# Two heads in one operand tile: scores of the first attention in 64x32 tiles of different halves of the array

## What is computed

```python
xn = _layernorm(x, axis=-1)
x = x + _L0_attn_ref(xn, ...) + _L0_ffn_ref(xn, ...)

# first branch: 16 heads of width 8, rotary positions, causal
scores = jnp.einsum('bqhd,bkhd->bhqk', q, k) / math.sqrt(Hd)
scores = jnp.where(causal, jnp.finfo(scores.dtype).min, scores)
attn = jax.nn.softmax(scores, axis=-1)
out = jnp.einsum('bhqk,bhkd->bhqd', attn, v)

# second branch: 6 nodes after each other, each an attention of 8 heads of width 16, not causal
o = _mha(q, k, v, Wq[c], Wk[c], Wv[c], Wo[c])
nodes[c] = act_w[c] * o + q
```

## Time and profile before

| | |
|---|---|
| median of 3 runs | 1426.18 us (1425.83 to 1427.39) |
| profiled execution | 1423.05 us, its span 1421.3 us |
| PE busy | 1380.5 us, 97% of the span |
| DVE busy | 1263.0 us, 89% |
| ACT busy | 1139.5 us, 80% |
| POOL busy | 449.8 us, 32% |

### The profile page before, as it was taken

The page is one execution under the profiler, slowest core; times in us unless marked ns, Lnnn a source line. Parts: engine busy times, 40 slices in busy tenths (PEclk is TensorE's granted clock), DMA queues, the critical chain, the costliest instruction groups (busy, mean ns, idle before and its releaser), DMA issues.

```text
span 1421.3 us, 60282 instructions
## 1 busy us (share of the span) xinstructions
PE 1380.5 (97%) x26216; PEld 935.3 (66%) x26216; DVE 1263.0 (89%) x1587; ACT 1139.5 (80%) x2133; POOL 449.8 (32%) x936
## 2 busy tenths in 40 slices
PE   6899999999999999999999999999999999999995
PEld 4467777656667666676676766766667666667652
DVE  8889999999989989899899898988989989989895
ACT  3378887688878878888788887887888878878784
POOL 5141115324422433233423332234233432330210
PEclk9899999999999999999999999999999999999998
DMA  8131112343232422333323323233233332321211
GB/s 253 47 116 60 51 59 98 119 142 119 81 127 70 132 97 77 102 109 107 104 78 114 107 74 121 83 123 107 69 101 107 101 107 80 127 98 56 76 38 40
DMA packets 115668, 137.68 MB, mean 97 GB/s; under 512 B 14972, under 2 KB 90109, under 8 KB 115277
## 3 DMA queue, kind: packets, MB, share of 16 engines
q1 hardware_dynamic: 115405, 133.83, 28.7%
HBM read 64.63 MB, written 61.98 MB: 89 GB/s over the span
## 4 chain that ended last, share of the span: by engine, by line
PE 88%; DMA 4%; DVE 3%; SPq 2%; ACT 1%; POOL 1%; issue 1%; ACTq 0%; POOLq 0%; DVEq 0%
PE s L1069 53%; PE cps L1163 26%; PE misc L1069 7%; DMA qs<-mrows 2%; DVE neg_max L971 1%; SPq L431 1%; PE misc L1064 1%; ACT probs L784 1%; DMA dram_raw_b<-csb 1%; PE s L1064 0%; DVE s L967 0%; POOL parts L601 0%; POOL ks L596 0%; POOL full L614 0%; SPq L500 0%
## 5 line engine op out<-in xcount | busy, mean ns | idle before, releaser
L784 ACT ACTIVATE probs<-s 128x512 f32<-128x512 f32 x1792 | 1059.2, 599 | 227.4 <-PE s L1069 166.8
L971 DVE TENSOR_REDUCE neg_max<-s 128x1 f32<-128x1024 f32 x768 | 936.5, 1222 | 62.0 <-PE s L1069 9.1
L1069 PE MATMUL s<-qs,ks 99*32 99x512 bf16 (+2 forms) x7680 | 808.4, 370 | 7.1 <-DMA qs<-mrows 5.1
L1069 PE MATMUL s<-ks,qs 96*32 96x512 bf16 (+2 forms) x7680 | 606.5, 369 | 6.3 <-DMA ks<-dram_qk_a 2.7
L1163 PE MATMUL cps<-probs,vs 128*32 128x256 f32 (+1 forms) x7552 | 591.4, 368 | 0.6 <-ACT probs L784 0.6
L1069 PEld LDWEIGHTS s<-qs,ks 99*32 99x32 bf16 x7680 | 235.8, 94 | 240.6 <-ACT probs L784 96.7
L1163 PEld LDWEIGHTS cps<-probs,vs 128*32 128x32 f32 x7552 | 316.4, 110 | 76.3 <-issue 17.0
L1069 PEld LDWEIGHTS s<-ks,qs 96*32 96x32 bf16 x7680 | 292.5, 97 | 88.6 <-issue 24.5
L633 POOL TENSOR_TENSOR mparts<-neg_max,zeros 128x8 bf16<-128x8 f32 x128 | 26.0, 203 | 796.0 <-DVE neg_max L971 654.3
L967 DVE CUSTOM_DVE_ANT_0 s<-s,mask_q 128x1024 f32<-128x1024 f32 (+7 forms) x256 | 187.8, 785 | 23.5 <-PE s L1069 14.8
L706 POOL TENSOR_TENSOR parts<-full,zeros 128x512 bf16<-128x512 f32 x48 | 61.4, 1280 | 52.2 <-DVE full L949 52.2
(11 more groups left out here) (134 smaller groups left out, 607.6 us busy)
## 6 DMA issues: line engine op xcount, KB each, us to landing
dram_qk_b<-parts SPq DMA_DIRECT2D x48, 384.0 KB, 3.2
qs<-dram_qk_b SPq DMA_DIRECT2D x96, 192.0 KB
ks<-dram_qk_b SPq DMA_DIRECT2D x96, 192.0 KB
dram_qk_b<-parts SPq DMA_DIRECT2D x48, 256.0 KB, 3.2
dram_raw_b<-csb SPq DMA_DIRECT2D x93, 128.0 KB, 4.3
dram_qk_b<-parts SPq DMA_DIRECT2D x48, 128.0 KB, 3.2
vsrc<-srcT SPq DMA_DIRECT2D x12, 512.0 KB, 3.1
ctx_b<-dram_raw_b SPq DMA_DIRECT2D x44, 128.0 KB
```

The lines of the kernel that those rows point to most:

```text
L784: nc.scalar.activation(buf[:, lo:hi], s2[bank][:, 0:hi - lo], ACT.Exp, scale=scale).then_inc(exp_done, 1)
L971: last = ve.tensor_reduce(peak, scores, AX.X, ALU.max, negate=True)
L1069: last = te.matmul(dst[c0:c0 + STRIP, :], lhsT[:, c0:c0 + STRIP], rhs, start=start, stop=stop, tile_position=(0, c0))
```

## The change

Head k and head k+2 of A share one operand tile. There are two such tiles of q (`qa`) and two of k (`ka`, laid over `ctx_b`, which is unused until B). Unit k lies in tile k % 2, in rows 0 to 50 or 64 to 114 (`first_row`): 48 rows of data and 3 for the maximum. Both scores of A are now strips of 64 rows and 32 columns, with `tile_position=(row, c0)`. Because units k and k-2 lie in different halves, the scores by query and by key of one step use different rows of the array. The mask on the diagonal can read only the 64 rows of its half; it takes the 32 columns of the identity in that half, and for output rows of the other half one of two further masks (`mask_far`). Operands of B, contexts and the transpose stay as they are. The data that DMAs move stays the same.

At the start, DVE clears no longer `qs` and `ks` but sets `ka` to ones; POOL writes the ones of `ks` before it waits for the statistics instead of at the end of its constants, and makes the two further masks.

```diff
+ROWS_A = 6 * DA
+HALF_ROWS = 64
...
+        mask_far = [sb(f"mask_far{n}", [128, 128], BF16) for n in range(2)]
+        qa = [sb(f"qa{n}", [128, S], BF16) for n in range(2)]
...
+        ka = [ctx_b[:, n * CH:(n + 1) * CH].bitcast(BF16) for n in range(2)]
...
+        def first_row(which, k):
+            return HALF_ROWS * (k % RING // 2) if which == "A" else 0
+        def operands(which, k):
+            return (qa[k % 2], ka[k % 2]) if which == "A" else (qs[k % RING], ks[k % RING])
+        def data_rows(which, k):
+            row = first_row(which, k)
+            return slice(row, row + (ROWS_A if which == "A" else KROW))
+        def score_rows(which, k):
+            row = first_row(which, k)
+            return slice(row, row + (ROWS_A if which == "A" else KROW) + 3)
...
-            sp.wait_ge(dve_const, 3 * RING)
+            sp.wait_ge(dve_const, RING + 2)
...
+            for s in range(RING):
+                pool.wait_ge(pool_const, 8 + s)
+                pl.memset(ks[s][MROW:128, :], 1.0).then_inc(pool_const, 1)
+            pool.wait_ge(pool_const, 8 + RING)
             for n in range(NB):
                 pool.wait_ge(ln_stats, n + 1)
...
+            for mask, key_of_row_0 in ((mask_k, 0), (mask_far[0], HALF_ROWS), (mask_far[1], -HALF_ROWS)):
+                pl.affine_select(out=mask[:, :], in_=mask[:, :], pattern=[[1, 128]], compare_op=ALU.is_ge,
+                                 fill=MASKED, base=-key_of_row_0, channel_multiplier=-1).then_inc(pool_const, 1)
...
-            for s in range(RING):
-                pool.wait_ge(pool_const, N_CONST - RING + s)
-                pl.memset(ks[s][MROW:128, :], 1.0).then_inc(pool_const, 1)
...
             for s in range(RING):
-                for ring in (qs[s][:, :], ks[s][:, :], vs[s][:, :, :]):
-                    ve.memset(ring, 0.0).then_inc(dve_const, 1)
+                ve.memset(vs[s][:, :, :], 0.0).then_inc(dve_const, 1)
+            for n in range(2):
+                ve.memset(ka[n][:, :], 1.0).then_inc(dve_const, 1)
...
-            def mm_strips(dst, lhsT, rhs, start=True, stop=True):
+            def mm_strips(dst, lhsT, rhs, start=True, stop=True, row=0):
                 for c0 in range(0, 128, STRIP):
                     last = te.matmul(dst[c0:c0 + STRIP, :], lhsT[:, c0:c0 + STRIP], rhs, start=start, stop=stop,
-                                     tile_position=(0, c0))
+                                     tile_position=(row, c0))
                 return last
+            def mask_strips(dst, row):
+                rows = slice(row, row + HALF_ROWS)
+                for c0 in range(0, 128, STRIP):
+                    here = c0 // HALF_ROWS == row // HALF_ROWS
+                    at, mask = (c0, mask_k) if here else ((c0 + HALF_ROWS) % 128, mask_far[row // HALF_ROWS])
+                    last = te.matmul(dst[c0:c0 + STRIP, :], ident_h[rows, at:at + STRIP], mask[rows, :],
+                                     start=False, stop=True, tile_position=(row, c0))
+                return last
...
-                    last = mm_strips(bank[:, first - lo:end - lo], ky[0:KALL, t * 128:(t + 1) * 128],
-                                     q[0:KALL, q0 + first - at:q0 + end - at], stop=not diagonal)
+                    last = mm_strips(bank[:, first - lo:end - lo], ky[rows, t * 128:(t + 1) * 128],
+                                     q[rows, q0 + first - at:q0 + end - at], stop=not diagonal, row=row)
                     if diagonal:
-                        last = mm_strips(bank[:, at - lo:at - lo + 128], ident_h[:, :], mask_k[:, :],
-                                         start=False)
+                        last = mask_strips(bank[:, at - lo:at - lo + 128], row)
...
-                                    last = mm_strips(s1[n % 2][:, lo:hi], q[0:KROW, t * 128:(t + 1) * 128],
-                                              ky[0:KROW, lo - at:hi - at])
+                                    last = mm_strips(s1[n % 2][:, lo:hi], q[rows, t * 128:(t + 1) * 128],
+                                                     ky[rows, lo - at:hi - at], row=row)
```

More of the change, by code:

```diff
@@ L197 @@
 FINISH = [(0, TB)] + [(TB + t0, tiles) for t0, tiles in LATE_TILES]
-N_CONST = 12 + 2 * RING
+N_CONST = 20 + RING
 def added(kind, r, k):
@@ L359, in head_row, with max_rows @@
             return here * HB + k if 0 <= k < UP else other * HB + k % UP
+        def first_row(which, k):
[8 more added lines that the diff above has]
+            return slice(row, row + (ROWS_A if which == "A" else KROW) + 3)
+        def max_rows(which, k):
+            return slice(data_rows(which, k).stop, score_rows(which, k).stop)
         block = ctx.enter_context(nc.Block())
@@ L429, in load_unit @@
                     need(sp, written, 4 * 3 * 16 * PREPS.after(kind, r))
-                for op, dst in ((0, qs[slot]), (1, ks[slot])):
-                    sp.dma_start(dst[0:6 * dims, :],
+                for op, dst in enumerate(operands(which, k)):
+                    sp.dma_start(dst[data_rows(which, k), :],
                                  qk_dram[which][op, :, bass.ds(row * dims, dims), :]
                                  ).then_inc(qk_in[slot], 16)
-            sp.wait_ge(dve_const, 3 * RING)
+            sp.wait_ge(dve_const, RING + 2)
             sp.wait_ge(pool_const, N_CONST)
@@ L519, in phase @@
                         sp.wait_ge(mrow_sb, u)
-                        sp.dma_start(qs[(k - 1) % RING][MROW:KALL, :].rearrange("a (i n) -> a i n", n=128),
+                        which = kind_at(kind, k, 1)
+                        sp.dma_start(operands(which, k - 1)[0][max_rows(which, k - 1), :
+                                                               ].rearrange("a (i n) -> a i n", n=128),
                                      mrows[(k - 1) % 2][:, :]).then_inc(mrow_in[(k - 1) % RING], 16)
@@ L567, in _ @@
             pl.memset(mask_q[:, :], 0.0).then_inc(pool_const, 1)
-            pl.memset(mask_k[:, :], 0.0).then_inc(pool_const, 1)
-            pool.wait_ge(pool_const, 3)
+            for mask in (mask_k, *mask_far):
+                pl.memset(mask[:, :], 0.0).then_inc(pool_const, 1)
+            pool.wait_ge(pool_const, 5)
             pl.affine_select(out=ident[:, :], in_=ident[:, :], pattern=[[-1, 128]], compare_op=ALU.not_equal,
@@ L572, in _ @@
             pl.memset(power[:, :], -0.5).then_inc(pool_const, 1)
-            pool.wait_ge(pool_const, 5)
+            pool.wait_ge(pool_const, 7)
             pl.tensor_copy(ident_h[:, :], ident[:, :]).then_inc(pool_const, 1)
+            for s in range(RING):
+                pool.wait_ge(pool_const, 8 + s)
+                pl.memset(ks[s][MROW:128, :], 1.0).then_inc(pool_const, 1)
+            pool.wait_ge(pool_const, 8 + RING)
             for n in range(NB):
@@ L586, in _ @@
             pl.memset(pick_sum[:, :], 0.0).then_inc(pool_const, 1)
-            pool.wait_ge(pool_const, 11)
+            pool.wait_ge(pool_const, 19)
             pl.affine_select(out=pick_sum[:, :], in_=pick_sum[:, :], pattern=[[-VW, 128 // VW], [0, VW]],
@@ L1277, in score_piece @@
                 which = kind_at(kind, k, 2)
-                q, ky = qs[(k - 2) % RING], ks[(k - 2) % RING]
+                q, ky = operands(which, k - 2)
+                rows, row = score_rows(which, k - 2), first_row(which, k - 2)
                 lo, hi = pieces(which, j)[n]
@@ L1309, in phase @@
                         if kind != "T":
-                            q, ky = qs[k % RING], ks[k % RING]
+                            q, ky = operands(kind[0], k)
+                            rows, row = data_rows(kind[0], k), first_row(kind[0], k)
                             if i == 0:
```

6 lines of the change are left out of this document (2 added, 4 removed).

## The result

The changed kernel takes 1430.39 us (median of 14 runs, 1423.50 to 1435.03), against 1425.70 (14 runs, 1420.38 to 1428.61) for the kernel before beside it: a ratio of 1.0029, 95% interval 1.0018 to 1.0041. The forecast said slower by 10.5. Direction and range held; size and, as the stages show, composition did not.

A forecast was written before the change was run, and what follows sets the result against it. PE was taken to bound the first attention's steps, the stretch changed. Terms: +9.2 (AL, AZ), +1.0 (A0), +1.0 (B0), -0.7 (start), sum +10.5 us, giving a median of 1436.7 us; range 1414 to 1448, the forecast's own 1431 to 1452.

The forecast's parts named there:

- Changes of shape: First attention's steps: ten changes of tile shape a step, each draining PE for 0.105 us, bounds 0 to 0.18.
- Overlap: First attention's steps: key and query scores in different halves run partly together, saving 0.46 us in turns 1 to 4.
- +9.2: AL and AZ: 24 steps going from 6.50 to 6.88 us each, together 9.2 us slower.
- The forecast's own serial step: First attention: halves don't run together but changes drain; 0.94 us more a step, steps of 7.4, total 1455; chance 0.08.
- The next limit: Turn 0 of a step: its 1.25 us is the way over ACT's exponentials to the freed bank, so it saves nothing.
- DVE's idle per head: First attention's steps: DVE's idle time per head grows from 0.45 to 0.8 us, with steps of about 6.9.
- B0: B0's first two steps: 20 changes of shape a step, 2.1 us each step, mostly hidden by DVE in one; +1.0 for both.
- A0: Six steps of A0 with key scores: about +0.17 us each, +1.0 together.
- The start: Start of the kernel: POOL's backlog, ending with its last low part at 30.0, shifts earlier; -0.3 to -1.1, taken as -0.7 us.
- The second attention: Four fifths of the time: keeps its instructions, steps as before, apart from B0's first two; difference 0.
- only a change in columns drains: First attention: a change in rows costs nothing, DVE becomes the bound, steps of 6.15 us, total 1416; chance 0.21.

The follow-up runs named there:

- without overlap: Changed kernel with units k and k-2 put in the same half, so their scores can't run together; shapes and changes stay: 1481.73 us, ratio 1.039.
- the old layout: Changed kernel with A0's eight heads in full-height tiles as before: 1436.65 us (1.0059); with the last two heads of A so too: 1427.59 us (1.0007).
- the filler: Changed kernel with 4 x 4 useless float32 strips of 512 columns on PE in the wait at B0's start: 1424.94 us, ratio 0.9988.

## Why the prediction was right in sign, by luck, and wrong in its sum

**Changes of shape: right.** Contexts start 0.10 us after the last strips have streamed, key scores 0.10 after the transpose. The price of 0.105, taken from the rotations, measured as 0.11 to 0.12 without overlap. The Trainium skill's rule (TensorEngine Tiling (Array Packing), Key Properties) that changing the mode drains the engine agrees with this; the transpose still costs no change of its own.

**Overlap: the step that failed.** "Matmuls start in program order", so "the query scores can start only when the mask has started" with a gain of "0.04 a turn". The row at 187.89 starts ahead of the one at 188.08. The mask waits for its own half and holds up nobody in the other one. So the query scores run beside the key scores for a whole piece in every turn, in turn 4 too, where the forecast had no pair to overlap and the gain is 0.22. What was priced at 0.46 a step is 1.29. With 0.46 the forecast step was 6.88; the serial step of 7.60 less 1.29 is the measured 6.31. The forecast's own serial step was 7.34, so 0.26 of the 0.83 too little in the overlap was hidden by changes priced too low; the remaining 0.57 a step, over the 24 steps of AL and AZ, made +9.2 into -4.5. The Trainium skill (TensorE: Matmul & The Clock Gate, Part 3, what overlaps and what doesn't) states that matmuls start in program order; here the trace speaks against it, and the measurement decides.

**The next limit: named, not followed.** The forecast knew that turn 0's 1.25 was the way over ACT. It did not ask where PE would meet the same limit once the turns were short. PE idles 0.19 us a step, ACT's banks end the waits, and DVE, at 5.94 of 6.39, is not the bound. The expectation that DVE's idle per head would grow to 0.8 was wrong with the step's length: it is 0.45, as before.

**B0: the term that was mis-sized, +1.0 for +10.7.** Its mechanism, twenty changes a step with DVE hiding most of one, is the smaller part: 2.3 us with the clock kept. The other 8.4 are the low clock, of which the forecast had nothing. A wait of 1.70 us ahead of B0 stood in the trace of before, at a clock of 1.00; that with the halves such a wait would cost the clock could not be read from it.

**A0: right by chance.** +1.0 was booked for six changes and +1.07 measured. In fact the low stretch grew from 10.24 to 23.89 us, of which the forecast had nothing: the second and third step, inside it, take 3.7 us more (8.95 and 10.89 against 7.70 and 8.43), and the four behind them 1.4 less instead of more. The number itself is within what executions differ by: A0 takes 64.30 to 66.50 us in the profiles with the old layout and 65.50 to 67.29 in those with overlapping halves.

**The start: right in size, its mechanism shown in part.** -0.7 booked, -0.65 measured. POOL's last low part, the term named, ends at 29.79 instead of 30.0, which is 0.21 of it; the first scores start at 37.22 instead of 37.87. Where the rest comes from is not shown.

**The second attention** kept its steps behind B0, as forecast; +1.27 is inside what the executions differ by.

So the slower result does not confirm the forecast's reason, and the sign was luck: with the wait ahead of B0 filled, the clock is kept and the same kernel is at 0.9988, not slower than before. By the forecast, the first attention's steps were to pay for their changes of shape; they are faster, by 4.5 us. The loss is at the ends: B0's first two steps and, hidden in A0's sum, the clock after the start. The rival "only a change in columns drains", the one on the other side, was wrong too, though its steps of 6.15 were nearer to the 6.31 than mine.

**What stays open.** What in the steps with halves makes the clock fall behind a wait, and why it then stays low while PE is busy all the time; whether the length of the low stretch depends on the shapes at B0; how A0's long low stretch could be shortened (work ahead of it did not do it); and why a load is late at the change of AL's passes in some executions.

## What to carry to other kernels

Price an overlap of two halves of the array by each half's own queue of work, not by the order of the program, and price each change of tile shape at 0.1 us. When such a change shortens PE's turns, look next for the bank that another engine still reads, because work that looks like overhead may be what fills that wait. Where PE waits in a stretch whose tiles change shape, look at the granted clock first: here it was worth 8 us, more than the change itself, and useless matmuls in the wait bought it back.

## What the runs showed of the hardware that I had not expected

- A matmul in one row half starts ahead of an earlier one that waits for the other half: 187.89 against 188.08. Two halves together save 1.29 of 7.60 us a step.
- The granted clock fell to 0.50 (1.2 GHz) at 264.45 and stayed there for 20.48 us, while PE was busy for 20.48 of them. It came after a wait of 2.08 us and 1.5 us of mixed shapes. Of 14 runs of the changed kernel, 13 had a mean clock of 0.975 to 0.981; the one with 0.987 took 1423.50, the fastest. With the filler the mean is 0.985 to 0.987, and the times are 1423.90 to 1427.41.
- The Trainium skill (TensorE: Matmul & The Clock Gate, HAM oscillation) ties the low clock to idle time of TensorE. The traces agree that there was a wait ahead of each fall between 100 and 310 us, and that filling it keeps the clock. But the waits here are shorter than the section's example, and their length doesn't decide alone: the kernel before has one of 1.70 us at the same place and keeps 1.00, while falls followed 1.09 and 0.81 us in steps with halves.
